# Transposing the wide probabilities by products with scaled diagonals, and one batch's router logits in four column groups

## What is computed

```python
def _L0_xattn_ref(q, k, v, mask, Wq, Wk, Wv, Wo, bo):
    ...
    dots = jnp.einsum('bhid,bhjd->bhij', qh, kh) * scale
    dots = jnp.where(mask[:, None, :, :], mask_value, dots)
    attn = jax.nn.softmax(dots, axis=-1)
    out = jnp.einsum('bhij,bhjd->bhid', attn, vh)
    ...
    return out @ Wo + bo

def _L0_ffn_ref(x, Wg, bg, W1, b1, W2, b2):
    logits = xf @ Wg + bg
    idx = jnp.argmax(jax.nn.softmax(logits, axis=-1), axis=-1)
    h = jax.nn.gelu(jnp.einsum('th,ehi->tei', xf, W1) + b1, approximate=False)
    y = jnp.einsum('tei,eih->teh', h, W2) + b2
    out = jnp.take_along_axis(y, idx[:, None, None], axis=1)[:, 0, :]
    ...

x = x + jnp.tanh(g_xattn[0]) * _L0_xattn_ref(_layernorm(x), ctx, ctx, mask, ...)
x = x + jnp.tanh(g_ffn[0]) * _L0_ffn_ref(_layernorm(x), ...)
```

## Time and profile before

| | us |
|---|---|
| median of the runs | 199.1 |
| the profiled execution | 200.14 |
| span of its instructions | 198.3 |
| PE busy in the span | 185.5 |
| VectorE busy | 123.5 |
| ScalarE busy | 104.9 |
| GpSimd busy | 89.5 |

### The profile page before, as it was taken

One profiled execution on the slowest core, in us unless ns is written; L12 is line 12 of the kernel. 1 busy time (PEld: TensorE's weight loads), 2 busy tenths in 40 slices (PEclk: granted clock), 3 DMA queues, 4 the chain that ended last, 5 costly groups with the idle time before them and its releaser, 6 DMA issues.

```text
span 198.3 us, 4265 instructions
## 1 busy us (share of the span) xinstructions
PE 185.5 (94%) x1412; PEld 136.2 (69%) x1412; DVE 123.5 (62%) x538; ACT 104.9 (53%) x376; POOL 89.5 (45%) x128
## 2 busy tenths in 40 slices
PE   7999999999899999999999899998999999999960
PEld 6994455666665444788895666765788899989940
DVE  3479576899996421154459999997833556355520
ACT  3243438899998112211427899997631263445410
POOL 6000002577778991000003899768810024776650
PEclk9999999999999999999999999999999999999996
DMA  4998008999999990480000101600000002353011
GB/s 134 335 369 284 0 3 265 319 287 315 298 317 266 206 326 20 146 279 1 0 2 3 55 27 54 198 0 0 3 0 2 0 3 76 110 153 109 34 53 31
DMA packets 22323, 25.19 MB, mean 127 GB/s; under 512 B 1987, under 2 KB 20877, under 8 KB 22160
## 3 DMA queue, kind: packets, MB, share of 16 engines
q1 hardware_dynamic: 19536, 21.83, 37.3%
q0 software_dynamic: 1152, 2.12, 3.2%
q10 hardware_dynamic: 1600, 0.84, 1.5%
HBM read 14.14 MB, written 11.68 MB: 130 GB/s over the span
## 4 chain that ended last, share of the span: by engine, by line
PE 69%; DVE 21%; issue 3%; ACT 2%; POOL 1%; POOLq 1%; DVEq 0%
PE s_bank L1729 14%; PE o_bank L1674 14%; DVE probs L1308 12%; PE s_bank L2035 8%; PE o_bank L2046 7%; PE s_bank L1769 5%; DVE oT L1335 4%; PE s_bank L1608 3%; PE s_bank L1639 2%; PE o_bank L1817 2%; PE o_bank L1799 2%; PE t_bank L1700 2%; PE s_bank L1844 2%; ACT probs L832 2%; PE s_bank L2024 1%
## 5 line engine op out<-in xcount | busy, mean ns | idle before, releaser
L649 POOL TENSOR_TENSOR probs<-probs,r_col 128x512 f32<-128x512 f32 x32 | 33.3, 1040 | 73.8 <-DVE r_col L1319 73.7
L832 ACT ACTIVATE probs<-probs,negm_run 128x160 f32<-128x160 f32 x128 | 53.0, 415 | 6.1 <-DVE negm_run L1308 5.9
L1308 DVE CUSTOM_DVE_ANT_0 probs<-s_bank,maskneg 128x160 f32<-128x160 f32 x128 | 33.3, 317 | 3.5 <-PE s_bank L1769 3.2
L1729 PE MATMUL s_bank<-xnT,wq_sb 128*128 128x512 f32 x64 | 29.0, 600 | 0.0
L1674 PE MATMUL o_bank<-wo_sb,oT 128*128 128x256 f32 x128 | 28.7, 380 | 0.0
L1674 PEld LDWEIGHTS o_bank<-wo_sb,oT 128*128 128x128 f32 x128 | 23.9, 190 | 3.5 <-issue 0.5
L832 ACT ACTIVATION_READ_ACCUMULATOR probs<-probs,negm_run 128x1 f32 x128 | 23.9, 187 | 0.0
L1769 PE MATMUL s_bank<-k_sb,q_sb 64*128 64x160 f32 x256 | 21.7, 306 | 0.0
L1729 PEld LDWEIGHTS s_bank<-xnT,wq_sb 128*128 128x128 f32 x64 | 11.7, 190 | 13.1 <-issue 12.8
L628 POOL DMA_INDIRECT out_dram<-oT x16 | 17.0, 1064 | 7.8 <-DVE oT L1256 5.9
L1769 PEld LDWEIGHTS s_bank<-k_sb,q_sb 64*128 64x128 f32 x256 | 18.0, 187 | 2.7 <-DVE negm_run L1308 1.5
(11 more groups left out here) (169 smaller groups left out, 299.6 us busy)
## 6 DMA issues: line engine op xcount, KB each, us to landing
sorted_rows<-empty_row SPq DMA_DIRECT2D x8, 1040.0 KB, 15.6
oT<-in_L_ffn_W_dram SPq DMA_DIRECT2D x1, 2048.0 KB, 18.2
q_sb<-in_L_ffn_W_dram SPq DMA_DIRECT2D x1, 2048.0 KB, 9.4
oT<-sorted_rows SPq DMA_DIRECT2D x1, 1040.0 KB, 5.2
oT<-sorted_rows SPq DMA_DIRECT2D x8, 130.0 KB, 2.3
wq_sb<-in_L_xattn_Wq_dram SPq DMA_DIRECT2D x2, 512.0 KB, 8.1
mask_sb<-in_mask_BxSxS_bk_dram SPq DMA_DIRECT2D x2, 512.0 KB, 8.9
wv_sb<-in_L_xattn_Wv_dram SPq DMA_DIRECT2D x1, 1024.0 KB, 10.8
```

The costliest lines, as they stand in the source:

```text
L649: nc.gpsimd.tensor_tensor(window_wide(u), window_wide(u), r.rearrange("p i h -> p (i h)") .unsqueeze(2).broadcast_to([P, 4, WIDE]), ALU.mu ...
L832: last = nc.scalar.activation(window_part(u, i, h), window_part(u, i, h), ACT.Exp, bias=negm_run[at], scale=-1.0, accum_out=l_run[at])
L1308: nc.vector.tensor_tensor_reduce(window_part(u, i, h), s_bank[u % 2][:, h, i * CK:i * CK + WK], maskneg[:, q, 0:WK], -SCALE, LARGEST, ALU. ...
L1729: last = nc.tensor.matmul(bank[m % 4], wq_sb[:, c, m * P:(m + 1) * P], xnT[:, c, b * N:(b + 1) * N], start=(c == 0), stop=(c == DC - 1))
```

## The change

**The wide probabilities** are no longer multiplied by GpSimd and then transposed by the identity. GpSimd makes, once, `fold`, a 128 x 64 matrix with a one where the row modulo 64 is the column, and for each unit and part `fold` times the reciprocals of the part's rows, 4 x 64 columns, into a spare piece of the same tile (`window_diag`). PE then multiplies the unnormalised probabilities, as weights as before, by that diagonal instead of by the identity: an ordinary product in the place of a transpose. The left part stays as it was.

**The logits of batch 0** are no longer made tile by tile. After the transposes of all four tiles, `batch_logits` makes them with the router's weights as weights, padded to 32 columns with zeros, one tile to a group of 32 PSUM partitions. VectorE copies the 128 x 128 result to SBUF (`take_logitT`), and PE transposes it back (`batch_logits_back`). The steps move from the projection into the key products of batch 1. GpSimd clears the padded tiles beforehand, and ScalarE's queue waits for that before it issues the two small loads into them.

```diff
@@ -129,6 +129,7 @@
     NOWHERE = T
+    LEFT_E = P // QT
...
@@ -149,8 +150,9 @@
         b2_sb = sb("b2_sb", [P, E, D])
-        wg_sb = sb("wg_sb", [P, DC, E])
-        bg_sb = sb("bg_sb", [P, E])
+        wg_sb = sb("wg_sb", [P, DC, LEFT_E])
+        bg_sb = sb("bg_sb", [P, LEFT_E])
+        logitT = sb("logitT", [P, P])
         bo_sb = sb("bo_sb", [P, D])
...
@@ -382,6 +387,9 @@
+        def window_diag(u):
+            return probs[:, u % PB].rearrange("p i h k -> p (i h k)")[:, 6 * WIDE:8 * WIDE].rearrange("p (n k) -> p n k", n=4)
         def window_left(u):
@@ -503,7 +511,7 @@
                 sp.dma_start(b2_sb[:], b2.unsqueeze(0).broadcast_to([P, E, D])).then_inc(s_b2, 16)
-                sp.wait_ge(empty_ready, 2)
+                sp.wait_ge(empty_ready, 4)
                 if later_too:
@@ -590,6 +598,8 @@
                                     pattern=[[1, P]], channel_multiplier=-1).then_inc(route_const, 1)
+            nc.gpsimd.memset(wg_sb[:], 0.0).then_inc(empty_ready, 1)
+            nc.gpsimd.memset(bg_sb[:], 0.0).then_inc(empty_ready, 1)
             nc.gpsimd.memset(empty_row[:, 0:TOKEN], 0.0).then_inc(empty_ready, 1)
@@ -641,13 +651,18 @@
             def normalise_window(b, also):
+                if b == 0:
+                    pool.wait_ge(ident_ready, E + 3)
+                    nc.gpsimd.tensor_tensor(fold[:], ident[:, 0:DH], ident[:, DH:P], ALU.add).then_inc(fold_ready, 1)
+                    pool.wait_ge(fold_ready, 1)
                 for u in range(PER):
                     job, a = u // 2, u % 2
                     r = r_col[:, u % PB]
                     pool.wait_ge(first.r_col_ready, b * PER + (u + 1))
-                    nc.gpsimd.tensor_tensor(window_wide(u), window_wide(u), r.rearrange("p i h -> p (i h)")
-                                            .unsqueeze(2).broadcast_to([P, 4, WIDE]), ALU.mult).then_inc(first.pn_ready, 1)
+                    nc.gpsimd.tensor_tensor(window_diag(u), fold[:].unsqueeze(1).broadcast_to([P, 4, DH]),
+                                            r.rearrange("p i h -> p (i h)").unsqueeze(2).broadcast_to([P, 4, DH]),
+                                            ALU.mult).then_inc(first.pn_ready, 1)
                     nc.gpsimd.tensor_tensor(left_probs[:, job % 2, :, a * DH:(a + 1) * DH]
@@ -781,8 +796,9 @@
             act.dma_start(bo_sb[:], bo.unsqueeze(0).broadcast_to([P, D])).then_inc(s_small, 16)
-            act.dma_start(bg_sb[:], bg.unsqueeze(0).broadcast_to([P, E])).then_inc(s_small, 16)
-            act.dma_start(wg_sb[:], wg.rearrange("(c p) e -> p c e", p=P)).then_inc(s_small, 16)
+            act.wait_ge(empty_ready, 2)
+            act.dma_start(bg_sb[:, 0:E], bg.unsqueeze(0).broadcast_to([P, E])).then_inc(s_small, 16)
+            act.dma_start(wg_sb[:, :, 0:E], wg.rearrange("(c p) e -> p c e", p=P)).then_inc(s_small, 16)
             done = act.alloc_register("act_done")
@@ -1148,13 +1164,21 @@
             left = dve.alloc_register("dve_left")
+            def take_logitT():
+                dve.wait_ge(logit_ps, 1)
+                nc.vector.tensor_copy(logitT[:], bank[5][:, P:2 * P]).then_inc(logitT_taken, 1)
             def route_logits(r):
                 R = routes[r]
                 at, tiles = ROUTED[r][0] % QT, ROUTED[r][1]
                 shape = [P, tiles, E]
-                logits = bank[5][:, at * E:(at + tiles) * E].rearrange("p (t e) -> p t e", e=E)
-                dve.wait_ge(logit_ps, r + 1)
+                if r == 0:
+                    logits = bank[5][:, 2 * P:3 * P].rearrange("p (t e) -> p t e", e=LEFT_E)[:, :, 0:E]
+                else:
+                    logits = bank[5][:, at * E:(at + tiles) * E].rearrange("p (t e) -> p t e", e=E)
+                dve.wait_ge(logit_ps, r + 2)
                 then(nc.vector.tensor_reduce(R.lmax[:], logits, AX.X, ALU.max))
...
@@ -1694,13 +1722,30 @@
                         nc.tensor.matmul(bank[5][:, q * E:(q + tiles) * E].rearrange("p (t e) -> p t e", e=E),
-                                         ones[0:1, :], bg_sb[0:1, :].unsqueeze(1).broadcast_to([1, tiles, E]),
+                                         ones[0:1, :], bg_sb[0:1, 0:E].unsqueeze(1).broadcast_to([1, tiles, E]),
                                          start=True, stop=False)
                 for c in range(DC):
-                    last = nc.tensor.matmul(bank[5][:, at], xnT[:, c, tt * P:(tt + 1) * P], wg_sb[:, c, :], start=False,
+                    last = nc.tensor.matmul(bank[5][:, at], xnT[:, c, tt * P:(tt + 1) * P], wg_sb[:, c, 0:E], start=False,
                                             stop=(tt in LAST_ROUTED and c == DC - 1))
                 if tt in LAST_ROUTED:
                     last.then_inc(logit_ps, 1)
+            def batch_logits():
+                pe.wait_ge(xt2_sb, QT)
+                by_tile = [bank[5][t * LEFT_E:(t + 1) * LEFT_E, P:2 * P] for t in range(QT)]
+                for t in range(QT):
+                    nc.tensor.matmul(by_tile[t], bg_sb[0:1, :], ones[0:1, :], start=True, stop=False)
+                for c in range(DC):
+                    for t in range(QT):
+                        last = nc.tensor.matmul(by_tile[t], wg_sb[:, c, :], xnT[:, c, t * P:(t + 1) * P], start=False,
+                                                stop=(c == DC - 1))
+                last.then_inc(logit_ps, 1)
+            def batch_logits_back():
+                pe.wait_ge(logitT_taken, 1)
+                nc.tensor.transpose(bank[5][:, 2 * P:3 * P], logitT[:], ident[:]).then_inc(logit_ps, 1)
@@ -1784,9 +1829,10 @@
                                 for r in range(2):
-                                    last = nc.tensor.transpose(bank[4 + r][:, at:at + DH],
-                                                               window_wide(u)[head_rows[r], 2 * i + h, :],
-                                                               ident[head_rows[r], head_rows[r]])
+                                    last = nc.tensor.matmul(bank[4 + r][:, at:at + DH],
+                                                            window_wide(u)[head_rows[r], 2 * i + h, :],
+                                                            window_diag(u)[head_rows[r], 2 * i + h, :],
+                                                            start=True, stop=True)
                     last.then_inc(first.ptrans_ready, 1)
@@ -1985,11 +2031,11 @@
                 if where == "k1":
-                    tile_logits(2)
+                    xn2_transposes(3)
                 elif where == "k2":
-                    xn2_transposes(3)
+                    batch_logits()
                 elif where == "k3":
-                    tile_logits(3)
+                    batch_logits_back()
                 elif where == "v0":
@@ -2107,14 +2153,12 @@
                         project_tile(2)
-                        tile_logits(0)
                         xn2_transposes(1)
                         project_tile(3)
                         if later_too:
                             context(first, b, b)
                         else:
                             window_context(b)
-                        tile_logits(1)
                         xn2_transposes(2)
```

More of the change, by code:

```diff
@@ L161, in flamingo_kernel @@
         ident = sb("ident", [P, P])
+        fold = sb("fold", [P, DH])
         ones = sb("ones", [P, P])
@@ L274, in flamingo_kernel @@
         ident_ready = sem("ident_ready")
+        fold_ready = sem("fold_ready")
         pool_step = sem("pool_step")
@@ L314, in flamingo_kernel @@
         logit_ps = sem("logit_ps")
+        logitT_taken = sem("logitT_taken")
         count_ready = sem("count_ready")
@@ L1400, in attend @@
                     nc.vector.tensor_copy(*k_dst(u + 1)).then_inc(S.k_dve, 1)
+                    also(f"k{u}")
                 dve.wait_ge(S.mask_ready, n + 1)
@@ L1442, in route_first_batch @@
             def route_first_batch(where):
-                if where == "k":
+                if where == "k1":
+                    take_logitT()
+                elif where == "k":
                     route_logits(0)
```

## The result

The changed kernel took **212.51 us** (median) against 199.04 of the kernel before, timed beside it: a ratio of 1.068, with an interval from 1.064 to 1.073. One of the four executions of the kernel before took 364.73 us; the ratio leaves it out. Forecast were 209.4 us, 5% slower, in a range of 205 to 217. So sign, cause and range held, and the forecast was 3.1 us too low. The profiled execution took 212.93 us with a span of 211.2, 12.9 more than the span of before.

A forecast was written before the change was run, and what follows sets the result against it. Two loops bound the attention beat, ScalarE's queue and PE to VectorE and back; PE had at most 0.29 us idle. Batch 0 +5.7, batch 1 +5.25, logits −0.7 sum to +10.3: 209.4 us, range 205 to 217.

The forecast's parts named there:

- The cause: Wide step on PE: each product is two records with own weight loads, 16 steps of 0.11 us instead of 8.
- The size of the beat: Attention, one job from left transposes to left transposes: 4.55 us against 3.86, +0.69 a beat.
- First to second values: Piece of PE's beat: 0.45 us, from 0.52 before less some of a wait for ScalarE's copy.
- No new wait, but no slack either: PE before first values: wide and left copies end some 1.2 us after left transposes may start, scores fill 0.17 + 1.14.
- The wide step: PE, per job: 16 steps of 0.11 us take 1.76 us, in the place of 1.01.
- Job 0 and job 7: First and last jobs of each batch's attention: +0.69 and +0.90 us in batch 0, +0.45 and +0.90 in batch 1.
- The logits: Batch 0's logits, moved into batch 1's key products: −0.7 us, with −1.2 and +0.4 as ends.
- GpSimd at nothing: GpSimd's shorter work, 0.61 instead of 1.04 us, frees 0.43 a unit and was counted as no gain.
- 0.14 a step: Rival: a wide step costs what the score row shows, 2.24 us a job, 217 us in all; chance 0.08.
- 0.06 to 0.07: Rival: wide steps cost as little as with transposes, beat stays 3.86, only logits count, 199 us; chance 0.08.
- load plus columns: Rival: loads can't run under products of the same rows, so columns add: 0.165 a step, 223.5 us; chance 0.05.
- GpSimd in the loop: Rival: GpSimd's multiplication is waited for, so 0.43 us comes off each of 16 beats, 192 us; chance 0.03.

The follow-up runs named there:

- the two halvings: The whole change with 32 instead of 64 moving columns in each wide product, 212.79 us; and with 64 instead of 128 weight columns, 199.72 us.
- The four single-part runs: Kernel before with new logits only, 199.42 us; with wide change only, 213.47; with products by identity for wide transposes, 213.43; whole change with transposes, 198.55.
- The run with ScalarE's copies: The whole change, but ScalarE copies both banks of the wide step and VectorE only the left one: 211.04 us, ratio 1.0557.

## Why the prediction was right, and where it was short

**The cause** held: two records to a product, a step of 0.112 us that, as far as the two halvings tell, the load sets (forecast 0.11, from the logits' loads), 16 of them in the place of 8, PE as the bound. The four single-part runs leave no other part that loses.

**The size of the beat** is the term that was too small: 4.77 instead of 4.55, in twelve beats 5.45 + 5.24 = 10.69 us instead of 8.04, 2.65 more. In the spans the whole miss is 12.9 − 10.3 = 2.6 us. The rest of the 3.1 lies between profiled executions and medians: the profiled execution of before lay 1.0 us over its median, which the forecast took off, and the one after only 0.4. The beat by its pieces:

- First to second values: 0.63, forecast 0.45, +0.18. Two steps of the working failed here. "No new wait, but no slack either" was a wait: the copies end 1.23 us after the left transposes start (57.21 to 58.44), and PE gets there after 0.12 + 1.14 = 1.26, with no time for the semaphore and the load. The run with ScalarE's copies shows the price, 0.13 a beat in all, of which 0.10 is in this piece. The other 0.08 was never a wait: the prediction took 0.07 off the 0.52 of before as ScalarE's copy, and 0.53 stays with the same 0.33 of idle loads whether the profile names that copy or nothing. What the two kinds of product do there, from tiles of 64 rows to tiles of 128, is a change of PE's tile shape. The Trainium skill says that such a change drains the engine ("TensorEngine Tiling (Array Packing)", section "Key Properties"); this would fit, but no run here changed the shape alone (see below).
- The wide step: 1.83 instead of 1.76, +0.07. Its first step, which follows products of the other tile shape, takes 0.16 and the rest 0.11.
- Scores to first values +0.03, left transposes to scores −0.05.

On the tile shape the kernel before has more to say. Its first values follow scores, which are also of 64 rows, in the middle of a batch; in job 7 of batch 0 they follow query products of 128 rows, and the copies that they wait for had ended 2 us earlier (VectorE's at 62.32, ScalarE's at 63.09). Their weight loads in both places, and the products of the second:

```profile
47.12 0.33 PEld L1811 LDWEIGHTS o_bank<-pT,v_sb 64*128 64x128 f32 x4
...
65.28 0.30 PEld L1811 LDWEIGHTS o_bank<-pT,v_sb 64*128 64x128 f32 x4 [0.76 <-issue]
...
65.28 0.70 PE L1811 MATMUL o_bank<-pT,v_sb 64*128 64x256 f32 x4
```

After scores the load begins 0.13 us ahead of its product (47.25); after query products it begins with it, and the first values take 0.70 instead of 0.59, with nothing to wait for. So where the tile shape changes, about 0.1 us is lost, as much as the late wait costs. The second values and the wide step are such places in each beat, before and after. That it is the shape is inferred from where this happens, and not tested.

**Job 0 and job 7**: +0.77 and +0.93 in batch 0 (forecast 0.69 and 0.90), +0.52 and +1.12 in batch 1 (0.45 and 0.90). The job 7 of batch 1 missed by the same step, "no new wait": PE stood 0.41 us at the wait for VectorE's copy (147.97). With ScalarE's copies this job fell from 4.77 to 4.29.

**The logits**: −0.63 after and −0.58 alone, forecast −0.7. The six rounds of four took 0.93 us instead of 0.67; the wait for the context copy, 0.24, is where it was expected.

**GpSimd at nothing** held within a per cent, not exactly: the run with the diagonals and transposes is some 1 us faster than the logits alone.

**The rivals**: 0.14 a step, 0.06 to 0.07, and load plus columns were excluded by the records (0.112) and by the two halvings; GpSimd in the loop by the run with transposes. Between 1.9 us for the wide step, the estimate by the Trainium skill's figure ("Terms", as above), and the 1.76 that the prediction took from rows, the measured 1.83 stands in the middle.

## What to carry to other kernels

A transpose by the identity and a product by a diagonal look alike in the code, but in fp32 the product is two records with a weight load each, here 0.95 us against 0.24 for eight; fold a scale into a transpose only where PE has that time free in the beat. Before moving work from an engine that waits (GpSimd waited 73.8 us here) to one that is nearly the bound, read the room of the receiver in that stage, 0.29 us a beat here. And a wait that is met 0.03 us late isn't free on PE: here it cost 0.13 us a beat, since the weights behind it were not loaded ahead. Of this change the logits part alone is worth keeping.

## What had not been expected of the hardware

- A wait in PE's queue that costs next to nothing in itself, 0.03 us, costs another 0.10 because the first weight load behind it starts with its product (58.50 for both).
- The step of fp32 products with 64 rows by 128 columns of weights is the same to 0.03 us in 16 steps with 64 and with 32 moving columns, and falls from 0.112 to 0.067 us with half the weight columns.
- The first wide product after products of another tile shape took 0.16 us in place of 0.11, and the first values 0.70 in place of 0.59 where they follow products of another shape.
